# Later loads, earlier sums, evictions by bank, and GpSimd's wide operations in pieces of 512 columns in the first batch

## The reference

```python
# mamba2
zxbcdt = einsum('bld,de->ble', x, w_in)          # z 1024, xBC 1280, dt 16 columns
xBC = silu(conv over 4 tokens of xBC)
y = ssd(xh * dt, dt * A, Bm, Cm) + xh * D        # 16 heads of 64, state of 128
y = y * silu(z)
y = y * rsqrt(mean(y * y) + EPS) * norm_w
return einsum('ble,ed->bld', y, w_out)
# ffn
hidden = silu(x @ W1.T) * (x @ W3.T)             # 2048 wide
hidden = fwht(hidden)                            # Walsh-Hadamard transform
return hidden @ W2.T
```

## Time and profile before

| what | us |
|---|---|
| median of 3 runs | 1002.84 |
| the runs | 1002.79 to 1005.53 |
| the profiled execution's own time | 1006.06 |
| its span | 1004.2 |

### The profile page before, as it was taken

The page is one execution under the profiler, slowest core; times in us unless marked ns, Lnnn a source line. Parts: engine busy times, 40 slices in busy tenths (PEclk is TensorE's granted clock), DMA queues, the critical chain, the costliest instruction groups (busy, mean ns, idle before and its releaser), DMA issues.

```text
span 1004.2 us, 13294 instructions
## 1 busy us (share of the span) xinstructions
PE 948.2 (94%) x4999; PEld 472.5 (47%) x5000; DVE 592.6 (59%) x963; ACT 353.9 (35%) x546; POOL 320.9 (32%) x358
## 2 busy tenths in 40 slices
PE   8799857998999999999999999999999999999997
PEld 3344423543444445454545445454545445544543
DVE  6875557776453667675551766675542766576521
ACT  6676645423323343332221433232221433232200
POOL 0001433645100204756410204665410205665410
PEclk9999978898999999999999999999999999999999
DMA  9678533514322535452322535443321535343122
GB/s 330 213 256 303 185 123 118 190 56 157 126 84 85 170 105 157 152 153 82 108 64 63 181 98 155 156 148 87 102 74 53 181 105 158 107 145 98 50 74 94
DMA packets 76206, 134.25 MB, mean 134 GB/s; under 512 B 7536, under 2 KB 20464, under 8 KB 74096
## 3 DMA queue, kind: packets, MB, share of 16 engines
q1 hardware_dynamic: 56640, 104.88, 32.6%
q10 hardware_dynamic: 19504, 28.53, 8.7%
HBM read 107.43 MB, written 25.95 MB: 133 GB/s over the span
## 4 chain that ended last, share of the span: by engine, by line
PE 77%; DVE 11%; issue 5%; ACT 3%; DMA 2%; POOL 1%; ACTq 0%; SPq 0%; DVEq 0%
PE ps L593 49%; PE ps L825 15%; PE ps L787 3%; DVE arena L1335 3%; PE ps L773 2%; PE ps L779 2%; DVE arena L1218 1%; PE ps L759 1%; DMA arena<-w_out 1%; PE ps L712 1%; PE ps L742 1%; DVE arena L1332 1%; ACT arena L911 1%; DVE arena L1165 1%; DVE arena L1234 1%
## 5 line engine op out<-in xcount | busy, mean ns | idle before, releaser
L593 PE MATMUL ps<-xh,arena 128*128 128x512 f16 x1592 | 496.2, 384 | 8.0 <-DVE arena L1165 5.1
L593 PE MATMUL ps<-xl,arena 128*128 128x512 f16 x796 | 306.3, 385 | 0.0
L593 PEld LDWEIGHTS ps<-xh,arena 128*128 128x128 f16 x1592 | 160.5, 101 | 200.0 <-issue 14.5
L825 PE MATMUL ps<-arena 128*128 128x512 f16 x768 | 171.1, 379 | 0.0
L1405 POOL TENSOR_TENSOR arena<-arena 128x512 f16<-128x512 f32 x64 | 71.0, 1109 | 280.4 <-ACT arena L961 280.4
L1415 POOL TENSOR_TENSOR arena<-arena 128x2048 f32<-128x2048 f32 x16 | 58.5, 3657 | 231.3 <-DMA arena<-cs_rows 230.8
L593 PEld LDWEIGHTS ps<-xl,arena 128*128 128x128 f16 x796 | 78.5, 99 | 90.5 <-issue 7.3
L1218 DVE SCALAR_TENSOR_TENSOR arena<-ps,cw,arena 128x511 f32<-128x511 f32 (+2 forms) x120 | 89.5, 748 | 48.4 <-ACT arena L951 46.5
L825 PEld LDWEIGHTS ps<-arena 128*128 128x128 f16 x768 | 74.2, 98 | 91.1 <-issue 5.5
L961 ACT ACTIVATE arena<-arena 128x512 f16<-128x512 f32 x64 | 40.4, 630 | 169.3 <-DVE arena L1239 169.3
L956 ACT ACTIVATE arena<-ps,f 128x512 f32<-128x512 f32 x64 | 43.4, 678 | 102.6 <-PE ps L593 102.6
(11 more groups left out here) (177 smaller groups left out, 1119.1 us busy)
## 6 DMA issues: line engine op xcount, KB each, us to landing
arena<-w_parts SPq DMA_DIRECT2D x198, 256.0 KB, 2.6
w_parts<-arena SPq DMA_DIRECT2D x66, 256.0 KB, 2.2
arena<-cs_rows ACTq DMA_DIRECT2D x16, 1024.0 KB, 6.2
arena<-w SPq DMA_DIRECT2D x24, 512.0 KB, 4.8
arena<-ecs_rows ACTq DMA_DIRECT2D x24, 256.0 KB, 4.0
arena<-x ACTq DMA_DIRECT2D x18, 256.0 KB, 3.2
w_mid<-arena SPq DMA_DIRECT2D x8, 512.0 KB, 3.4
arena<-w_mid SPq DMA_DIRECT2D x16, 256.0 KB, 2.7
```

The source lines that it names most:

```text
L593: ins = nc.tensor.matmul(out_ap, lhs(i, a), rhs(i, c), start=(i == 0 and s == 0), stop=(i == n - 1 and s == 2))
L825: ins = nc.tensor.matmul(bank(t), hw[a][:, i, t * P:(t + 1) * P], w2s[i % W2R][:, d, :], start=(i == 0 and s == 0), stop=(i == JF - 1 and ...
```

## The change

Six edits. (1) In batch 0 SP meets the load of `w_out` (WOL) before tile Z7 and no longer behind A0, and ACT's squares of it (WOQ) stand one tile earlier. (2) Sums: WOS goes from place 11 to 10, and no longer waits for the scale of group 4; QS3 and QS4 change places with tiles, and QS4 waits for `scale_wo`. (3) Item L is gone in every batch: `csbc` is loaded in item E, right ahead of `ecsb`. (4) In batch 0 items of chunks 1 to 3 stand up to one tile later. (5) The last item G takes its banks in the order 0 to 3 and signals each, and OUT waits for each bank alone. (6) In batch 0 GpSimd's subtraction is issued as four instructions and its 1024-column operations as two each.

```diff
-FIRST_AT = ([("WOL", 0, 1)] + [("WOQ", q, q + 2) for q in range(8)] + [("WOS", 0, 11)] +
+FIRST_AT = ([("WOQ", q, q + 1) for q in range(8)] + [("WOS", 0, 10)] +
...
                         elif i == 7:
-                            pe.wait_ge(yscl_ok.sem, yscl_ok.at(0, 1))
+                            pe.wait_ge(mamba_evac.sem, mamba_evac.at(0, 0))
...
+                        if i == 4:
+                            pe.wait_ge(scale_wo, 1)
...
                     elif kind == "WOS":
-                        pe.wait_ge(scale_13, 5)
+                        pe.wait_ge(scale_13, 4)
...
                     elif kind == "V":
                         pe.wait_ge(sqr_ok.sem, sqr_ok.at(b, c))
-                        if b == 0 and c < 2:
-                            pe.wait_ge(scale_13, 6 + 2 * c)
+                        if b == 0 and c == 1:
+                            pe.wait_ge(scale_13, QUADS)
...
-                        for t in (0, FREE_BANK, 1, 2):
+                        for t in (0, FREE_BANK, 1, 2) if i < JF - 1 else range(NC):
...
+                            if i == JF - 1 and t < NC - 1:
+                                ins.then_inc(down_done.sem, 1)
...
-                    elif kind == "L" or (kind == "E" and c == 0):
+                    elif kind == "E":
...
-                    elif kind == "E":
-                        act.wait_ge(d_cst, (b + 1) * 32)
-                        act.wait_ge(t1_ok.sem, t1_ok.at(b, c - 2))
-                        for r in range(2):
...
+                        if c > 0:
+                            act.wait_ge(t1_ok.sem, t1_ok.at(b, c - 2))
+                            for r in range(2):
...
                     elif kind == "QS":
                         dve.wait_ge(quad_sums, i + 1)
+                        if i in (4, 7):
+                            dve.wait_ge(pe_tot.sem, pe_tot.at(0, i // 7))
+                        elif i == 5:
+                            dve.wait_ge(pe_mean.sem, pe_mean.at(0, 0))
...
                     elif kind == "OUT":
-                        dve.wait_ge(w2_used.sem, w2_used.at(b, JF - 1))
                         dve.wait_ge(mamba_evac.sem, mamba_evac.at(b, NC - 1))
                         for t in range(NC):
+                            if t < NC - 1:
+                                dve.wait_ge(down_done.sem, down_done.at(b, t))
+                            else:
+                                dve.wait_ge(w2_used.sem, w2_used.at(b, JF - 1))
...
+        def pieces(b, n, k):
+
+            k = k if b == 0 else 1
+            return [slice(i * (n // k), (i + 1) * (n // k)) for i in range(k)]
...
-                        nc.gpsimd.tensor_tensor(Eb, csbc, cs_s[:, c * NH:(c + 1) * NH].unsqueeze(2).to_broadcast([P, NH, P]),
-                                                ALU.subtract).then_inc(esub_ok.sem, 1)
+                        cs_c = cs_s[:, c * NH:(c + 1) * NH].unsqueeze(2).to_broadcast([P, NH, P])
+                        for h in pieces(b, NH, 4):
+                            ins = nc.gpsimd.tensor_tensor(Eb[:, h], csbc[:, h], cs_c[:, h], ALU.subtract)
+                        ins.then_inc(esub_ok.sem, 1)
```

More of the change, by code:

```diff
@@ L59 @@
     "R": (8, 16, 24, 35),
-    "L": (None, 3, 9, 17),
     "E": (None, 6, 14, 22),
@@ L1424, in _ @@
                         pool.wait_ge(diag_read.sem, diag_read.at(b, c - 1))
-                        nc.gpsimd.tensor_tensor(XD.rearrange("p (q l) -> p q l", q=QE), XT[:, 0:QE, c * P:(c + 1) * P],
-                                                dcol[:].unsqueeze(2).to_broadcast([P, QE, P]), ALU.mult).then_inc(xd_ok.sem, 1)
+                        for q in pieces(b, QE, 2):
+                            ins = nc.gpsimd.tensor_tensor(XD.rearrange("p (q l) -> p q l", q=QE)[:, q], XT[:, 0:QE, c * P:(c + 1) * P][:, q],
+                                                          dcol[:].unsqueeze(2).to_broadcast([P, QE, P])[:, q], ALU.mult)
+                        ins.then_inc(xd_ok.sem, 1)
                         if c < NC - 1:
                             pool.wait_ge(xdt_ok.sem, xdt_ok.at(b, c))
-                            nc.gpsimd.tensor_tensor(Xdec.rearrange("p (h d) -> p h d", h=NH), Xdt.rearrange("p (h d) -> p h d", h=NH),
-                                                    dec[:, c * NH:(c + 1) * NH].unsqueeze(2).to_broadcast([P, NH, HD]),
-                                                    ALU.mult).then_inc(xdec_ok.sem, 1)
+                            dec_c = dec[:, c * NH:(c + 1) * NH].unsqueeze(2).to_broadcast([P, NH, HD])
+                            for h in pieces(b, NH, 2):
+                                ins = nc.gpsimd.tensor_tensor(Xdec.rearrange("p (h d) -> p h d", h=NH)[:, h],
+                                                              Xdt.rearrange("p (h d) -> p h d", h=NH)[:, h], dec_c[:, h], ALU.mult)
+                            ins.then_inc(xdec_ok.sem, 1)
                     elif kind == "ROW":
@@ L1448, in _ @@
                         pool.wait_ge(xd_ok.sem, xd_ok.at(b, c))
-                        nc.gpsimd.tensor_tensor(XD, XD, t1, ALU.add).then_inc(t2_ok.sem, 1)
+                        for h in pieces(b, E, 2):
+                            ins = nc.gpsimd.tensor_tensor(XD[:, h], XD[:, h], t1[:, h], ALU.add)
+                        ins.then_inc(t2_ok.sem, 1)
                         if c < NC - 1:
-                            nc.gpsimd.tensor_tensor(state.rearrange("p (h d) -> p h d", h=NH), state.rearrange("p (h d) -> p h d", h=NH),
-                                                    tot[:, c * NH:(c + 1) * NH].unsqueeze(2).to_broadcast([P, NH, HD]),
-                                                    ALU.mult).then_inc(sdec_ok.sem, 1)
+                            tot_c = tot[:, c * NH:(c + 1) * NH].unsqueeze(2).to_broadcast([P, NH, HD])
+                            for h in pieces(b, NH, 2):
+                                state_h = state.rearrange("p (h d) -> p h d", h=NH)[:, h]
+                                ins = nc.gpsimd.tensor_tensor(state_h, state_h, tot_c[:, h], ALU.mult)
+                            ins.then_inc(sdec_ok.sem, 1)
 def constants():
```

13 lines of the change are left out of this document (7 added, 6 removed), and 2 rows, old and new, of the table FIRST_AT.

## The result

The median fell from 1004.18 us (1002.79 to 1005.64, 4 runs) to 988.73 (987.80 to 989.30, 4 runs): a ratio of 0.9845, 95% interval 0.9824 to 0.9866. The forecast was 981, so of the 21.9 us that it promised some 15.5 came. The profiled execution has a span of 987.5 us (before 1004.2) and took 989.29 itself. By the end of the last down matmul of each batch on PE, batch 0 is 7.1 us shorter (320.97 for 328.07), batch 1 3.7 (220.90 for 224.61), batch 2 2.1, batch 3 1.9, and the evictions behind the last matmul 1.9. Batches 1 to 3 and the end did what was forecast; batch 0 gave about half of the 13 us forecast for it.

The account below looks back on a forecast made before the run. It took PE's idle and half-speed time in batch 0 as the bound, batches 1 to 3 being all PE. Terms 13 (A to C, 14.0 by sum) + 7 + 1.9 = 21.9 us off 1002.84 gave 981; range 969 to 993.

Parts of the forecast that it names:

- What bounds it: Batch 0, 84 to 330 us: PE busy 213.2 of 246, granted clock 0.92; batches 1 to 3 all PE.
- Term A: Load of `w_out` in batch 0 issued 4.55 us earlier, so ACT has it sooner: 2.5 us, bounds 0 and 5.3.
- Term B: Batch 0's 11 us gap at WOS goes, smaller gaps at QS4 and QS5 remain: 11.0 us, bounds 5.4 and 13.5.
- Term C: Pieces and the rest of batch 0, chunk 3's later load counting against: 0.5 us, bounds -4 and +10.0.
- The walk: Batch 0's timeline carried forward with the gains so far: 4.5 us gap at H0, which gains 4.7 over Term B.
- the prediction's signs: Among them: no DVE split over 1.9 us in batch 0; wrong if GpSimd's pieces take over 1.3 us each.
- Term D: Batches 1 to 3: later `csbc` load frees the gating, PE stops waiting for ACT's square: 7 us, bounds 0 and 7.5.
- Rival 3: Load of `csbc` takes 12.57 us, `Xdec` late in batches 1 to 3: 32.7 us lost, 1014 us; chance 0.04.
- Term E: End of the program: with banks in order the last evictions finish sooner behind the last matmul: 1.9 us.
- Rival 1: DVE and ACT carry batch 0, the gap only moves: Term B 5.4, Term A and Term C 0; 988.5 us; chance 0.18.
- Rival 2: Late subtraction in batches 1 to 3 blocks another two-input DVE operation, Term D 0: 988 us; chance 0.11.
- rival 4: GpSimd's operations in batch 0 don't get split, a scheduler putting pieces back together; given no chance.

Follow-up runs that it names:

- the two other executions of the same batch 0: Changed kernel with loads of batches 1 to 3 early (996.38 us), and with last evictions as before (990.15 us); batch 0 up to its evictions unchanged in both.
- the better order: Changed kernel with chunk 3's load of batch 0 early and W1 a tile later: 979.75 us, ratio 0.9746; with whole GpSimd operations 989.54 us, 0.9831.

## Why the prediction was right and wrong

The median, 988.7, lies between the two bounds of 969 and 993, but 1.7 us above the 974 to 987 that the forecast kept for itself. In the profile the gain is 16.8 us for 21.9: 7.1 for 13 in batch 0, 7.8 for 7 in batches 1 to 3, 1.9 for 1.9 at the end. So the forecast missed in batch 0 alone.

- **What bounds it**: right. All of the gain but 0.9 us of batch 1 is where the waits of the earlier trace rows and the end of the earlier trace rows were.
- **Term A, forecast 2.5**: near in size, wrong in its place. Nothing was gained before WOS (A4's eviction is 0.2 us earlier: the squares stand before A2's split, and A2, U2 and QS3 wait 1.4, 1.9 and 1.4). The gain comes at WOS, which waits 0.2 us in place of 3.3 in the run with the sums alone: at A7 the changed kernel leads that run by 2.2 us, and by 1.5 without its pieces. The load at its old place, with the squares still early, costs 2.8 there. Only the profiles show these sizes.
- **Term B, forecast 11.0**: the mechanism was right to about a microsecond (QS4 at 135.8 after 2.9 of wait, forecast 2.1; QS5 at 147.6 after 4.6, forecast 148.5 after 5.7). The mis-sized step is the sentence "A7 starts at 150.7, where it started at 161.75. B is 11.0." It started at 149.87, sooner still; but the sum compares two starts, and the slow tile that lay ahead of V0 before (156.45 to 161.1) lies behind it now. The prediction priced such a tile behind QS6 and H0 and forgot it behind QS5: 2.5 us. A and B together measured 9.4, not 13.5; B alone, without the early load, 6.3 to 6.7.
- **Term C, forecast 0.5**: it measured 9.4 - 7.1 = 2.3 us of loss, and 9.1 - 8.8 = 0.3 in the two other executions of the same batch 0. The walk saw the wait at H0 (4.5 forecast, 3.0 to 3.4 came, with a slow tile behind it in one execution of three). It missed N2. The failed step is that V2's 4.1 us and its slow tile simply go. The chain root, W1, Y2, square stood in this order before, with 5.03 us of DVE waiting in it, and ended just as PE came to N2. In the changed kernel PE came 9.2 us sooner and the chain only 4.8, and the wait of 4.7 us that this makes was in no sum of the prediction: it had named who is blocked by GpSimd's length, not who stands behind a waiting instruction in DVE's list. Putting W1 behind Y2 brought 6.8 us (0.9845 to 0.9777), and with chunk 3's load early 10 us.
- **The pieces**: a split took 902 ns for 1165 (a free one 750), and only 124 of the 263 are the pieces' (1026 without them); the rest came with the other edits, though not with the sums (1216 in the run with these alone). GpSimd's price was more than forecast (6.8 us more busy from 84 to 330 for 4.4), though an undisturbed subtraction in four pieces costs 0.43 us more (4.04 for 3.61), 0.14 an instruction and not 0.19. Two of the prediction's signs were missed narrowly: one split of batch 0 took 2.00 us (limit 1.9), and single pieces of the sum in S took up to 1.71 (limit 1.3). That they are worth nothing that can be told here and 8.5 us in the better order was in neither theory.
- **Term D, forecast 7**: right, 7.8 in the profile (4.9 to 10.5 over the eleven executions with late loads, 7.7 on average) and 6.3 by the run with early loads. The same run gave the six waits back. Two small points were off: batch 1 gained 3.7 and not 2.5 (0.9 of it isn't in any wait, and stays open), and chunk 2 broke its limit: loads of 8.52 and 8.71 us were enough, though 9.1 was the forecast, since `Xdec` then took 3.92 us. Rival 3 thus exists, at 2.8 us for two chunks and with no slow tile behind them (PE has the full clock in batches 2 and 3), not at 32.7. By its own terms it would eat the gain from a load of 10.8 us on, not 11.5.
- **Term E, forecast 1.9**: 2.77 - 0.89 = 1.88.
- **Rival 1** gave 988.5, nearly the time that came, for a reason that fell. It said that DVE and ACT can't carry batch 0 any faster, so that the gap only moves. Gaps did stand at QS4, QS5, QS6, N2 and H0. But moving W1 by one tile and one load back took 8.0 to 9.7 us more out of batch 0 with the same instructions on DVE and ACT: it was the order in their lists. That the median came within 1 us of this rival's sum is chance, since its terms (B 5.4, A and C 0) aren't those measured. Rival 2 is out (no wait in batch 1), and so is rival 4.

Two things stay open. Of the pieces' 8.5 us, 5.0 are waits from 150 to 235; how much of the rest is a slow tile that is avoided, no run shows. And the prediction took 2.5 us of slow tile behind every gap of some 3 us: behind the 2.9 to 3.4 us at H0 it came in one of three executions, and no run says on what it hangs.

## What to carry to other kernels

When a gap is removed, add up to the end of the first tile that runs slow behind the next gap, not to a start: a slow tile that changes sides is part of the sum. When one engine is made to come sooner, go through the other engines' lists for waits that cost nothing so far, and ask of each chain behind them whether it comes sooner by as much; here one such chain (root, W1, Y2, square) took more back than the early load of `w_out` gave. A change that looks worthless in one order (the pieces) should be tried again once the wait behind it is gone. Before a slow tile is put down to an edit, look at other executions of the same instructions.

## What was unexpected in the hardware

- Two DVE instructions on 128x8 numbers waited for GpSimd's pieces as wide ones do. They stood beside S2's pieces (207.60 to 212.5) and took 1.18 and 0.97 us:

```profile
209.38 1.18 DVE L1291 TENSOR_TENSOR f_had<-f_had 128x8 f32<-128x8 f32 x1
210.59 0.97 DVE L1293 TENSOR_SCALAR f_had<-f_had,scl 128x8 f32<-128x8 f32 x1
```

In the kernel before, with GpSimd at rest, they took 0.17 and 0.23 us; beside the whole operations of the run without pieces the first took 1.82.
- Whole operations keep DVE out longer but let GpSimd end sooner; at each seam DVE can get in, and then GpSimd waits. Four pieces took 4.04 to 4.49 us in place of 3.61 in the changed kernel, and 5.12 once with chunk 3 early and W1 later. Two whole operations have such a seam too: `Xdec` in batch 2, right behind `XD`, took 3.92 us for 1.90 while DVE's product of 2048 columns, begun just before it, took 3.07 for 2.29.
- GpSimd's time for 1024 float32 columns depended on the second operand: 1.90 us where it is a few columns, each repeated along the row (lines 1425, 1429, 1451), and 2.34 at the least where it is a full tile (line 1449, 12 times in the kernel before).
- The same matmul at H0, in the same list, took 2.04 us behind a wait of 2.99 and 1.10 behind waits of 3.04 and 3.43 in other executions, and once, with the load of `w_out` late, 2.05 behind one of 2.38. The granted clock was 0.50 from 234 to 240 in the first and 1.00 in the next two; 3 us hung on it. So the length of the wait alone doesn't say whether PE comes back slow.
